# A graph network's third pass: the pair normalisation is split over two steps of VectorE, TensorE's sum of a pair follows the send, and block sums are added first in a step

## The reference

```python
h = jnp.maximum(_layernorm(x, axis=-1), 0.0)
x = x + _L0_gnn_ref(h, ...)            # relations: h_rel[src, rel_type] * norm, summed by dst
h = jnp.maximum(_layernorm(x, axis=-1), 0.0)
x = x + _L1_gnn_ref(h, ...)            # Chebyshev: Tx1 = prop(Tx0), Tx2 = 2*prop(Tx1) - Tx0
h = jnp.maximum(_layernorm(x, axis=-1), 0.0)
x = x + _L2_gnn_ref(h, ...)            # attention over edges, 86 relations
h = jnp.maximum(_layernorm(x, axis=-1), 0.0)
x = x + _L3_gnn_ref(h, src, dst)       # mean over neighbours
```

## The kernel before, in words

| engine | step 0 | step 1 | step 2 | step 3 |
|---|---|---|---|---|
| VectorE | | | `end_pair` | whole `norm_pair` |
| ScalarE | `turn_pair`, piece 0 | piece 1 | piece 2, `stage_pair` | piece 3, `root_pair` |
| TensorE | piece 1 | piece 2, `sum_pair` ahead of the `send` | piece 3, `turn_pair` | piece 0 |

## Time and profile before

### The profile page before, as it was taken

How to read it: one execution, slowest core, us unless ns; L and a number is a source line. 1 busy time by engine, 2 the same in 40 slices (tenths; PEclk the granted TensorE clock), 3 DMA queues, 4 the chain that set the end, 5 groups by cost and what they waited for, 6 DMA issues and landing times.

```text
span 8363.1 us, 145338 instructions
## 1 busy us (share of the span) xinstructions
PE 5338.8 (64%) x39187; PEld 4254.1 (51%) x39188; DVE 4727.0 (57%) x15433; ACT 2564.9 (31%) x8163; POOL 5380.2 (64%) x5577
## 2 busy tenths in 40 slices
PE   5333333333276777777777777777777777786666
PEld 2222222222255555655545554477777777775555
DVE  5555555565588888644444444344444444448885
ACT  4444444444322222233333333312111111123221
POOL 2777777777577777444444443177777777766775
PEclk9555555555567666655555555555555555558997
DMA  6000000000122222234444434422222222213332
GB/s 160 14 14 14 14 14 14 14 14 14 24 52 51 51 51 51 63 134 139 136 140 143 144 133 137 142 41 41 41 41 41 41 41 41 41 35 86 88 88 59
DMA packets 463911, 542.65 MB, mean 65 GB/s; under 512 B 219394, under 2 KB 373026, under 8 KB 463710
## 3 DMA queue, kind: packets, MB, share of 16 engines
q0 software_dynamic: 178288, 148.77, 11.3%
q1 hardware_dynamic: 228973, 178.17, 8.1%
q10 hardware_dynamic: 56448, 213.62, 6.4%
HBM read 293.47 MB, written 246.66 MB: 65 GB/s over the span
## 4 chain that ended last, share of the span: by engine, by line
POOL 41%; PE 22%; issue 19%; DVE 7%; DVEq 5%; ACTq 2%; ACT 2%; DMA 1%; POOLq 0%; SPq 0%
POOL arena L690 41%; PE ps_agg L1083 6%; PE ps_wide L1310 5%; PE ps_agg L1204 3%; PE ps_wide L1188 2%; DVE tbuf L1760 2%; DVEq L1800 2%; PE ps_t L1310 2%; DVE msg L1799 1%; ACTq L1013 1%; PE ps_wide L1191 1%; ACT tbuf L1008 1%; DMA arena<-table,ibuf 1%; DVEq L1525 1%; PE ps_z L1288 1%
## 5 line engine op out<-in xcount | busy, mean ns | idle before, releaser
L690 POOL DMA_INDIRECT arena<-table,ibuf x3328 | 3155.1, 948 | 1240.1 <-issue 1144.9
L690 POOL DMA_INDIRECT arena<-nodes,ibuf x2240 | 2222.4, 992 | 1638.7 <-DVEq L1538 789.2
L1083 PE MATMUL ps_agg<-mem_a,arena 128*32 128x80 f32 (+1 forms) x3904 | 524.0, 321 | 570.9 <-DVEq L1525 558.7
L1083 PE MATMUL ps_agg<-mem_b,arena 128*32 128x80 f32 (+1 forms) x3904 | 476.6, 301 | 504.0 <-DVEq L1525 464.8
L1083 PEld LDWEIGHTS ps_agg<-mem_a,arena 128*32 128x32 f32 (+1 forms) x3904 | 461.9, 164 | 629.2 <-DVEq L1525 577.4
L1083 PEld LDWEIGHTS ps_agg<-mem_b,arena 128*32 128x32 f32 (+1 forms) x3904 | 417.4, 152 | 561.4 <-DVEq L1525 492.3
L1760 DVE TENSOR_SCALAR tbuf<-iota,at_f 128x256 bf16<-128x256 bf16 x2940 | 631.1, 299 | 0.5 <-PE ps_t L1204 0.3
L813 ACT ACTIVATE tbuf<-O,tbuf 128x49 bf16<-128x49 bf16 x2176 | 586.4, 363 | 118.0 <-DVE H L1675 118.0
L1341 PE MATMUL ps_agg<-tbuf,msg 128*64 128x80 f32 x2496 | 373.6, 344 | 330.4 <-DVE msg L1967 330.4
L1310 PE MATMUL ps_wide<-w2f,ht 33*128 33x462 f32 (+2 forms) x1078 | 557.0, 785 | 30.2 <-ACT tbuf L1008 30.2
L955 ACT ACTIVATE att<-score 128x8 f32<-128x8 f32 x208 | 43.3, 208 | 1650.1 <-DVE score L1958 1650.1
(11 more groups left out here) (379 smaller groups left out, 11206.0 us busy)
## 6 DMA issues: line engine op xcount, KB each, us to landing
table<-tbuf ACTq DMA_DIRECT2D x294, 544.5 KB
idx_a<-lows_d SPq DMA_DIRECT2D x602, 192.0 KB
arena<-table,ibuf POOLq DMA_INDIRECT x3328, 2.5
table<-tbuf ACTq DMA_DIRECT2D x98, 495.0 KB
arena<-nodes,ibuf POOLq DMA_INDIRECT x2240, 2.9
table<-tbuf SPq DMA_DIRECT2D x25, 1024.0 KB, 4.3
idx_a<-lows_d SPq DMA_DIRECT2D x86, 224.0 KB
nodes<-O SPq DMA_DIRECT2D x7, 224.0 KB, 3.0
```

Of the source, the lines that this page charges most:

```text
L690: nc.gpsimd.indirect_dma_start(out=INTO[s][:, k, c, 0:WIDTH[s]], out_offset=None, in_=TABLE[s], in_offset=bass.IndirectOffsetOnAxis(ap=ibu ...
L1083: last = nc.tensor.matmul(ps_agg[ROW0[s]:ROW0[s] + CHN[s], 0:WIN], narrow[:, k, c, 0:CHN[s]], onehots[b][:, c, :], start=(c == 0), stop=(c ...
```

## The change

Three things move within the third pass, and nothing is added or taken away in arithmetic.

1. `norm_pair` is cut in two. `vary_pair` (lines 1921 to 1935) runs at the end of VectorE's steps with `q % 4 == 0`, `norm_pair` (the rest) at the end of the steps with `q % 4 == 1`. `root_pair` moves to ScalarE's steps 0, `turn_pair` and the four pieces move along on both engines.
2. TensorE's `sum_pair` stands behind the `send` of a step 1 in place of ahead of it.
3. `add_block` stands early in VectorE's step 2, right behind `compare_sources`, in place of behind `add_group`.

| engine | step 0 | step 1 | step 2 | step 3 |
|---|---|---|---|---|
| VectorE | `vary_pair` | `norm_pair` | `end_pair` | |
| ScalarE | piece 2, `root_pair` | piece 3 | `turn_pair`, piece 0, `stage_pair` | piece 1 |
| TensorE | piece 3, `turn_pair` | piece 0, `sum_pair` behind the `send` | piece 1 | piece 2 |

The loops that run on after the last block get two more steps, as pairs are finished later. The core of the diff:

```diff
 # ScalarE, pick_weighed
-                            if q % 4 == 0 and (q >= 8 or not first):
+                            if q % 4 == 2 and not first:
                                 next_part(act, rooted, turned, turn_pair)
-                            if (q >= 8 or not first) and q < NBATCH + 4:
-                                next_piece(act, (q - 4) % 4, turned, built, build_piece)
-                            if q % 4 == 2 and (q >= 6 or not first):
+                            if not first and q < NBATCH + 6:
+                                next_piece(act, (q - 2) % 4, turned, built, build_piece)
+                            if q % 4 == 2 and (q >= 6 or not first) and q < NBATCH + 4:
                                 next_pair(act, i * TURN + (f + q // NBATCH) * TURN, made, stage_pair)
-                            if q % 4 == 3 and (q >= 7 or not first):
+                            if q % 4 == 0 and not first:
                                 next_part(act, made, rooted, root_pair)
 # TensorE, pick_weighed
-                        if s == 2 and (q >= 7 or not first):
-                            next_piece(pe, (q - 3) % 4, turned, built, build_piece)
+                        if s == 2 and not first:
+                            next_piece(pe, (q - 1) % 4, turned, built, build_piece)
                         if q + 3 < NBATCH or not last:
                             pick(i, f, q + 3)
-                        if s == 2:
-                            norm_parts(i, f, q, first)
+                        if s == 2 and q % 4 == 0 and not first:
+                            next_part(pe, made, turned, turn_pair)
                         if q in HIDDEN[s]:
                             multiply_group(s, i, HIDDEN[s][q], f)
                         send(i, f, q)
+                        if s == 2 and q % 4 == 1 and (q >= 5 or not first):
+                            next_pair(pe, i * TURN + f * TURN, made, sum_pair)
 # VectorE, pick_weighed
                         if goes(q + 1):
                             compare_sources(i, f, q + 1)
+                        if s == 2 and q % NBATCH == 2 and (q >= NBATCH or not first):
+                            add_block(i, f + q // NBATCH - 1)
...
-                        if q % NBATCH == 2 and (q >= NBATCH or not first):
+                        if s == 1 and q % NBATCH == 2 and (q >= NBATCH or not first):
                             add_block(i, f + q // NBATCH - 1)
                         if s == 2 and q % 4 == 2 and (q >= 6 or not first):
                             next_pair(dve, i * TURN + (f + q // NBATCH) * TURN, made, end_pair)
-                        if s == 2 and q % 4 == 3 and (q >= 7 or not first):
-                            next_part(dve, made, normed, norm_pair)
+                        if s == 2 and q % 4 == 0 and not first:
+                            next_part(dve, made, varied, vary_pair)
+                        if s == 2 and q % 4 == 1 and not first:
+                            next_part(dve, varied, normed, norm_pair)
```

More of the change, by code:

```diff
@@ L856, in goes @@
                         return (q >= 0 or not first) and (q < NBATCH or not last)
-                    for q in range(NBATCH + (5 if last else 0)):
+                    for q in range(NBATCH + (7 if last else 0)):
                         at = ((BEFORE[h] + f) * NBATCH + q) + i * NBATCH
@@ L1224, in pick_weighed @@
                         send(i, f, q)
+                        if s == 2 and q % 4 == 1 and (q >= 5 or not first):
+                            next_pair(pe, i * TURN + f * TURN, made, sum_pair)
                     if s == 2 and last:
[L1226 to L1234, removed]
+                        for q in range(NBATCH, NBATCH + 5):
+                            next_piece(pe, (q - 1) % 4, turned, built, build_piece)
+                            if q % 4 == 0:
+                                next_part(pe, made, turned, turn_pair)
+                            if q % 4 == 1:
+                                next_pair(pe, i * TURN + (f + q // NBATCH) * TURN, made, sum_pair)
                 def pick_turn(i, f, last):
@@ L1742, in pick_and_sum @@
                 if s == 2:
-                    made, normed = dve.alloc_register("dve_made"), dve.alloc_register("dve_normed")
-                    dve.reg_mov(made, 0)
-                    dve.reg_mov(normed, 0)
+                    made, varied, normed = [dve.alloc_register(f"dve_{n}") for n in ("made", "varied", "normed")]
+                    for r in (made, varied, normed):
+                        dve.reg_mov(r, 0)
                 def compare_sources(i, e, q):
@@ L1789, in pick_weighed @@
                         compare_sources(i, f, 0)
-                    for q in range(NBATCH + (4 if last else 0)):
+                    for q in range(NBATCH + ((6 if s == 2 else 4) if last else 0)):
                         if goes(q + 1):
                             compare_sources(i, f, q + 1)
+                        if s == 2 and q % NBATCH == 2 and (q >= NBATCH or not first):
+                            add_block(i, f + q // NBATCH - 1)
                         if q < NBATCH:
@@ L1888, in end_and_norm @@
                         end_pair(t)
+                        vary_pair(t)
                         norm_pair(t)
@@ L1911, in end_pair, with two, vary_pair @@
                 dve.sem_inc(s_final, 1)
-            def norm_pair(t):
-                def two(a):
-                    return a.rearrange("p (a c) -> p a c", a=2)
+            def two(a):
+                return a.rearrange("p (a c) -> p a c", a=2)
+            def vary_pair(t):
                 xt, of = X[:, bass.ds(t * (2 * D), 2 * D)], O[:, bass.ds(t * (2 * D), 2 * D)]
@@ L1935, in norm_pair @@
                 V.tensor_scalar(tdev[:, :], tdev[:, :], 1.0 / D, EPS, ALU.mult, ALU.add).then_inc(s_tvar, 1)
+            def norm_pair(t):
+                of = O[:, bass.ds(t * (2 * D), 2 * D)]
                 dve.wait_ge(s_tstd, t + 1)
```

## The result

The changed kernel takes 8130.46 us (median of 4 runs, 8123.4 to 8140.69) against 8361.67 us of the kernel before on the same chip (4 runs): ratio 0.9723, 95% interval 0.9711 to 0.9734, or 231 us less. The forecast was 8088 us, in a range of 8010 to 8210. The profiled execution's own time is 8131.57 us, its span 8129.8.

The account below looks back on a forecast made before the run. TensorE was taken as the bound, kept from its work by the pair normalisation. Terms -164 - 71 - 58 + 21 + 10 - 10 = -272 us gave 8093 us for the profiled execution, 8087 for the median, taken as 8088; range 8010 to 8210.

Parts of the forecast that it names:

- 1a: Split normalisation on VectorE: TensorE's pick no longer waits for the compare, -164 us; its send newly waits for the split part, +21.
- 2: `sum_pair` behind the send on TensorE: its wait for `sums_t` falls from 2.2 to .9 us a pair, -58 us.
- 3: `add_block` early in VectorE's step 2: hidden, so the send's wait of 3 us per turn goes, -71 us.
- the clock: TensorE's granted clock in the third pass: no wait right behind step 0's multiply, -10 us, between +20 and -75.
- the tail: After the last send, two more pieces are still to be made than before: +10 us, between +4 and +25.
- The test: Register test on VectorE before the compare behind `vary_pair`, taken at .3 us from idle stretches of .31.
- the pick's entry: Sign in the trace after: TensorE's `pick` waits for VectorE in the pair stretch come to under 30 us.
- half-of-it rival: VectorE and ScalarE turn late where covers are 1 to 2 us; 3 us a pair lost, -134 us, 8225; chance 0.16.
- rival of the higher clock: TensorE's higher clock holds in the third pass, ScalarE then bounds: 7770, in part 7900 to 8000; chance 0.08.
- slower rival: `sum_pair` blocks TensorE's next piece while stores hold ScalarE in piece 0; at 8 us +92, 8450; chance 0.07.

Follow-up runs that it names:

- e2: Changed kernel with edits 2 and 3 undone, so only the split of `norm_pair` against the kernel before: 8258.37 us, ratio 0.9869.
- e4: Changed kernel with `norm_pair` straight after `vary_pair` in VectorE's step 0, so it waits for the root again: 8224.95 us, 0.9826 to the kernel before.
- e9: Changed kernel with `vary_pair` ahead of `add_group` in VectorE's step 0, on a chip with 8366 us before: 8022.26 us, 0.9589 to the kernel before.
- e3: Changed kernel with `sum_pair` ahead of the `send` again, all else as changed: 8183.87 us, 0.9776 to the kernel before.
- e1: Kernel before with only edit 3, `add_block` early in VectorE's step 2: 8255.75 us, 0.9864 to the kernel before.
- e12: Changed kernel with `add_block` late again, on a chip where the kernel before takes 10897.08 us: 0.9868 to the kernel before.
- e5: Changed kernel with `vary_pair` ahead of `add_group` in VectorE's step 0, on a chip with 10889.91 us before: 0.9833 to the kernel before.

## Why the prediction was right, term by term

The mechanism was the forecast one: TensorE is the bound, and the waits taken off it make up most of the 231 us. The sizes, over the stretch of pairs:

| term of the sum | forecast | measured | shown by |
|---|---|---|---|
| 1a, pick's wait for the compare | -164 | -120 (164.4 to 44.2) | waits; e2, e4 |
| 1a, new wait of the send for the split part | +21 | +52 (4.9 to 56.4) | waits; e2, e9 |
| 2, the sum's wait for `sums_t` | -58 | -57 (99.4 to 42.4) | waits; e3 |
| 3, the send's wait for `add_block` | -71 | -71 | waits; e1 |
| waits for copies of the pieces | 0 | +20 (35.3 to 55.5) | waits |
| the clock | -10 | -58 of busy time, some 7 of it the matmuls outside | windows; e1 |
| the tail | +10 | +8 | the two traces; e2 |

The forecast column adds up to -272, the measured one to -226; some 7 us more lie in smaller waits and outside the pass, which makes the 233 us between the two profiled executions.

The rows of the trace gave the waits of terms 2 and 3 and the tail within 2 us. The tail belongs to the split: from the last block sum to the first gather e1 has 66.1 us, e2 74.7. The root had no wait left in the stretch, as worked out. The block sum was hidden: no `send` waits for it.

Three terms were mis-sized. The clock was taken at -10 with a bound of -75, and measured -50 to -58. I saw the gap of 3 us behind the multiply and did not price it, and e1 shows that closing it alone was worth 40 us beyond its own length. Term 1a was worked out with TensorE at 1.2 GHz throughout. There the compare behind `vary_pair` is ready .8 us before its pick. VectorE kept to that: with M, the end of the multiply, at 4218.12 us, it started the compare at M+3.65 (forecast 3.5) and had the last split part at M+6.54 (forecast 6.5). The test took .66 us, where the sum had .31 and .3. TensorE did not keep to it. At 2.4 GHz the piece ahead takes 2.8 us and not 3.7, and TensorE meets VectorE unready: .8 us at the pick and 1.0 at the send, the two lines of the timeline. The third are the waits for copies of the pieces, which the sum left out.

The trace of before could have told this. The earlier trace rows have the clock at 1.00 from 4246 to 4248 us, in the very piece 0 that the sum charges at 1.2 GHz, and from 4260 to 4266 us it is 1.00 too (the lines under e1). The errors belong together: a faster TensorE turns part of its gain into waits for the other engines. That they partly cancel is luck: the waits of 1a and the copies fell short by 95 us, and the clock gave 40 to 48 us more.

That the edits overlap shows in the parts: alone or singly undone they are worth 111 (e1), 109 (e2) and 53 us (e3), 273 in all, and together 231. Put in one after the other, they add: 0.0131 for the split (e2), 0.0093 for the block sum on top of it (e3), 0.0053 for the sum's place, 0.0277 in all. So the overlap lies between the split and the block sum, and the profiles put it down to the clock: the block sum's wait is 71 us either way, but only alone did closing it bring TensorE's busy time down with it. Why the clock gave nothing more beside the split these runs don't show.

Of the signs on record, one failed: the pick's entry was to be under 30 us and is 44.2. The others came: no wait of VectorE for `tsq` or `tdev` in the stretch, no `send` that waits for `add_block`, .9 us in front of the sum, a turn of 65.2 us, a clock under .7.

The half-of-it rival named the right place (the compare behind `vary_pair`) at a price too high: 44.2 us and the 51.5 us more in front of the send are 2.1 us a pair and not 3, and 16 of the 44.2 have another cause (e9). The rival of the higher clock rested on the Trainium skill, "TensorE: Matmul & The Clock Gate", section "HAM oscillation — how this bites in real kernels": waits between bursts of matmuls throttle the array each time, and without them it stays at full rate. The trace supports its direction (0.58 to 0.61, and 0.65 in e9) and not its end. In the turn shown no wait of TensorE is over 1.5 us, and the clock's mean is still 0.61. The slower rival did not come about: `sum_pair` waits .9 us, as worked out from ScalarE's chain.

## What to carry to other kernels

Where an engine waits for another's multiply, put its independent work in front of that wait and not behind it: moving `vary_pair` ahead of `add_group` was worth 1.3%, nearly half of what the whole change was. When engines run in lockstep by steps, work out for each moved part when its neighbours want it at both levels of TensorE's clock: here a cover of .8 us was gone once TensorE ran at 2.4 GHz. And do not take a wait at its length: the same 71 us were worth 111 us alone and 74 to 78 beside the split, and 118 us of added waiting cost 86 to 94 (e4).

## What the runs showed of the hardware that I had not expected

In three of the comparisons the kernel before took 8362 to 8367 us, in two others, each on a chip of its own, 10890 and 10897 us. On those chips single instructions last as long as elsewhere (the matmuls of line 1114 take 270 ns in the middle in e12 and in the kernel before, a gather's issue 945 and 948 ns), but TensorE does not get them back to back. From the trace of e12, in a row of 32 matmuls that wait for nothing after the first (start, duration, line, tiles, count, idle before):

```profile
1002.32 3.08 PE L1114 MATMUL ps_z<-tbuf,O 128*128 128x245 bf16 x24
...
1007.50 0.27 PE L1114 MATMUL ps_z<-tbuf,O 128*128 128x245 bf16 x1 [1.13 <-issue]
...
1008.23 0.27 PE L1114 MATMUL ps_z<-tbuf,O 128*128 128x245 bf16 x1 [0.46 <-issue]
...
1008.95 0.27 PE L1114 MATMUL ps_z<-tbuf,O 128*128 128x245 bf16 x1 [0.46 <-issue]
```

24 of them go in 3.08 us, and then most come one in .72 us, with idle time that nothing in the profile accounts for. ScalarE has it too: in front of its line 813 it stands idle 324 us without a releaser in e12, and not at all in the kernel before. What holds the engines up these runs don't show. Moves of this kind are worth less there: one and the same kernel saves 1.7% on such a chip (e5) and 4.1% elsewhere (e9).
